# Stage two by halves of tokens, expert sums handed over bank by bank, and the pick table moved, in an eight-stage transformer kernel

## The reference, cut to what matters

```python
x = x + tanh(g_xattn[0]) * wkv(td, tf, layernorm(x), ctx)                  # L0 attention: a scan
x = x + tanh(g_ffn[0])   * moe8_top2_plus_shared(layernorm(x))             # L0 FFN
x = x + tanh(g_xattn[1]) * masked_softmax_attention(layernorm(x), ctx)     # L1 attention
x = x + tanh(g_ffn[1])   * L1_ffn(layernorm(x))                            # 32 experts, top 4
x = x + tanh(g_xattn[2]) * attention_32_heads(layernorm(x), ctx)           # L2 attention
x = x + tanh(g_ffn[2])   * dense_moe8(layernorm(x))                        # L2 FFN, 8 experts x 256
x = x + tanh(g_xattn[3]) * int8_attention_16_heads(layernorm(x), ctx)      # L3 attention
x = x + tanh(g_ffn[3])   * dense_moe8_top_p(layernorm(x))                  # L3 FFN, 8 experts x 512
```

## Time and profile before

| | before |
|---|---|
| median of 3 runs | 1008.02 us (1006.38 to 1008.49) |
| the profiled execution's own time | 1007.44 us |
| its span, first to last instruction | 1005.6 us |
| PE busy / weight load | 854.8 us (85%) / 529.0 us |
| DVE / ACT / POOL busy | 675.8 / 521.0 / 327.2 us |
| mean granted PE clock | 0.942 of full |

### The profile page before, as it was taken

How to read it: one execution, slowest core, us unless ns; L and a number is a source line. 1 busy time by engine, 2 the same in 40 slices (tenths; PEclk the granted TensorE clock), 3 DMA queues, 4 the chain that set the end, 5 groups by cost and what they waited for, 6 DMA issues and landing times.

```text
span 1005.6 us, 17167 instructions
## 1 busy us (share of the span) xinstructions
PE 854.8 (85%) x6369; PEld 529.0 (53%) x6369; DVE 675.8 (67%) x1402; ACT 521.0 (52%) x840; POOL 327.2 (33%) x267
## 2 busy tenths in 40 slices
PE   5977999867457877887988998789799899999997
PEld 3434665554335666564544554455455556555654
DVE  7995889778856777274345579767777657744444
ACT  4714345444336887155568743664456885523332
POOL 2531333322674555203035662101355334100000
PEclk9978999987768999897679999999999999999999
DMA  8974443310247776502013453111465445433332
GB/s 270 330 261 119 120 122 110 89 48 1 99 152 232 255 233 189 185 33 64 2 45 114 127 179 106 48 49 33 126 189 158 127 127 160 155 97 109 95 104 80
DMA packets 60191, 129.12 MB, mean 128 GB/s; under 512 B 9267, under 2 KB 25025, under 8 KB 60114
## 3 DMA queue, kind: packets, MB, share of 16 engines
q1 hardware_dynamic: 55506, 119.17, 38.6%
q0 software_dynamic: 4608, 8.94, 2.4%
HBM read 83.95 MB, written 48.27 MB: 131 GB/s over the span
## 4 chain that ended last, share of the span: by engine, by line
PE 42%; DVE 18%; issue 18%; POOL 8%; ACT 7%; DMA 5%; SPq 1%; POOLq 0%; DVEq 0%; ACTq 0%
PE ps L1465 15%; PE ps L1481 7%; DMA arena<-seats 4%; POOL W L770 3%; PE ps L1829 2%; PE ps L1552 2%; PE ps L1815 2%; DVE x L2318 2%; PE ps L1749 1%; POOL W L773 1%; PE ps L1408 1%; POOL arena L714 1%; PE ps L1567 1%; DVE stats L2036 1%; POOL wb L773 1%
## 5 line engine op out<-in xcount | busy, mean ns | idle before, releaser
L1465 PE MATMUL ps<-turned_buf,W 128*128 128x512 f16 x576 | 135.2, 385 | 4.0 <-ACT ctx_sb L1024 1.7
L2302 DVE SCALAR_TENSOR_TENSOR ctx_sb<-ps,ctx_sb 128x512 f32<-128x512 f32 x96 | 66.2, 689 | 102.8 <-PE ps L1465 75.7
L1465 PE MATMUL ps<-turned_buf,wb 128*128 128x512 f16 x576 | 132.6, 379 | 2.6 <-DVE ctx_sb L2302 2.0
L2309 DVE TENSOR_TENSOR ctxT<-ctx_sb,ctxT 128x512 f16<-128x512 f32 x96 | 69.6, 726 | 63.7 <-ACT ctxT L1032 63.2
L770 POOL TENSOR_SCALAR W<-W 128x768 f32<-128x768 f32 x32 | 69.3, 2167 | 129.3 <-ACT wb L1044 67.2
L1032 ACT ACTIVATE ctxT<-ctx_sb 128x512 f16<-128x512 f32 x96 | 60.2, 627 | 91.1 <-DVE ctx_sb L2302 90.9
L1024 ACT ACTIVATE ctx_sb<-ps 128x512 f32<-128x512 f32 x96 | 57.2, 596 | 96.3 <-PE ps L1465 96.1
L1465 PEld LDWEIGHTS ps<-turned_buf,W 128*128 128x128 f16 x576 | 55.9, 100 | 67.1 <-issue 7.1
L1408 PE MATMUL ps<-turned_buf,W 128*128 128x512 f16 x360 | 86.7, 394 | 2.5 <-issue 2.5
L1465 PEld LDWEIGHTS ps<-turned_buf,wb 128*128 128x128 f16 x576 | 55.4, 98 | 62.2 <-DVE ctx_sb L2302 3.0
L758 POOL DMA_INDIRECT slots<-arena x64 | 62.3, 973 | 49.4 <-ACT arena L1095 37.7
(11 more groups left out here) (411 smaller groups left out, 1704.9 us busy)
## 6 DMA issues: line engine op xcount, KB each, us to landing
W<-in_w SPq DMA_DIRECT2D x77, 384.0 KB, 3.6
seats<-k_st SPq DMA_DIRECT2D x8, 1152.0 KB, 10.9
arena<-seats SPq DMA_DIRECT2D x32, 288.0 KB
kept<-W SPq DMA_DIRECT2D x24, 384.0 KB, 4.1
kept<-wb SPq DMA_DIRECT2D x24, 384.0 KB, 4.2
W<-kept SPq DMA_DIRECT2D x24, 384.0 KB, 3.0
wb<-kept SPq DMA_DIRECT2D x24, 384.0 KB
wb<-in_w SPq DMA_DIRECT2D x18, 384.0 KB, 3.9
```

What stands on the lines that cost most here:

```text
L1465: last = nc.tensor.matmul(bank(4 + n), w4[k % 4][:, w, n * D + c * P:n * D + (c + 1) * P], x16[:, i, c, half * HALF:(half + 1) * HALF], st ...
L2302: nc.vector.scalar_tensor_tensor(h_g[:, g % 2, :], bank(5), 1.0 / WSCALE, h_s[:, g % 2, :], ALU.mult, ALU.mult).then_inc(sem("gated"), 1)
L2309: nc.vector.tensor_tensor(h_16[:, g % 2, 1, :], h_g[:, g % 2, :], h_16[:, g % 2, 0, :], ALU.subtract)\
```

## The change

1. **Stage two by halves.** Keys are turned in groups of 4, 2, 6, 4 instead of 6, 6, 4, the first four through banks 1 and 3 only; half 0 of xn goes to PE after them, then half 0's scores, then two keys, then half 1. DVE: add half 0, statistics 0, add half 1, normalise 0, statistics 1, normalise 1; then the four steps of half 0, down_lo and the mask's largest, sums 0, the four steps of half 1, add 0, statistics 0, sums 1, add 1, statistics 1. POOL casts the mask between the two powers.
2. **One power for the RMS norm.** DVE gives POOL the variance times (1 + 1e-6) plus 1e-11, so that one power makes `rms`; the plain `rstd`, needed later, is made from a second variance for all eight tiles after the norm.
3. **Places.** `m_cum + m_base` is added before the counts; the mask instruction joins the one that writes the places; m_to is made and signalled in halves of four tiles, and POOL starts after the first.
4. **Dense passes.** DVE signals `out_read` after two tiles and after four; PE waits for the first before bank 6 and for the second before bank 7.
5. **picks** moves from step 6 to step 0 of half 0, with a wait for all of L2 attention's results.
6. **Rounding** of the norm in L3 attention: two tiles in step 6 and two in step 7, instead of four in step 7.
7. **Stores**: half 1 of the result in two pieces of two tiles.
8. Semaphores are merged (names only).

```diff
-        KEY_BANKS = (0, 1, 2, 3, 0, 1, 4, 5, 6, 7, 4, 5, 6, 7, 4, 6)
-        KEY_GROUPS = (6, 12, 16)
+        KEY_BANKS = (1, 3, 1, 3, 0, 2, 4, 5, 6, 7, 4, 5, 6, 7, 4, 6)
+        KEY_GROUPS = (4, 6, 12, 16)
...
+            for lo, hi in ((0, 4), (4, 6), (6, 8)):
+                sp.wait_ge(sem("out_read"), 2 * (EXPERTS_AT[2 + lo // 4] + E3) - hi % 4 // 2)
+                sp.dma_start(out.rearrange("b s d -> s b d")[:, lo:hi, :], x[:, lo:hi, :]).then_inc(sem("out_done"), 16)
...
-                    if s == 3:
...
+                    into = rms if s == 3 else rstd
+                    nc.gpsimd.tensor_tensor(into[:, sl], veps[:, sl], mhalf[:, sl], ALU.pow).then_inc(sem("ln_rstd"), 1)
...
-            inv_sqrt(2)
+            inv_sqrt(2, (0,))
             link(nc.gpsimd.tensor_copy(a1_mask, mask8[:, :, :]))
             nc.gpsimd.tensor_scalar(a1_neg, a1_mask, -1.0, 1e30, ALU.add, ALU.mult).then_inc(sem("mask"), 1)
+            inv_sqrt(2, (1,))
             inv_sqrt(3)
+            pool.wait_ge(sem("plain_var"), 1)
+            nc.gpsimd.tensor_tensor(rstd[:, :], veps[:, :], mhalf[:, :], ALU.pow).then_inc(sem("plain_rstd"), 1)
-            pool.wait_ge(sem("seat"), 2)
             for i in range(TOP1):
                 for t in range(B):
+                    if i == 0 and t % 4 == 0:
+                        pool.wait_ge(sem("seat"), 2 + t // 4)
...
             def picks():
+                pool.wait_ge(sem("x_2"), B)
-                    if s == 6 and h == 0:
+                    if s == 0 and h == 0:
                         picks()
...
@@ ACT @@
+            turned(2, xT_of, (0,))
             down_hi(1, 0)
-            turned(2, xT_of)
+            for n in range(KEY_GROUPS[0], KEY_GROUPS[1]):
+                key_out(n)
+            turned(2, xT_of, (1,))
...
@@ PE, half_down @@
                 for t in range(4):
+                    if first and g and t % 2 == 0:
+                        pe.wait_ge(sem("out_read"), 2 * (EXPERTS_AT[p] + k // per) - 1 + t // 2)
@@ PE, stage two @@
-            pe.wait_ge(sem("key_ready"), KEY_GROUPS[0])
-            turn(2)
             for h in range(2):
+                if h:
+                    for n in range(KEY_GROUPS[0], KEY_GROUPS[1]):
+                        turn_keys(n)
+                    pe.wait_ge(sem("key_ready"), KEY_GROUPS[0])
+                turn(2, halves=(h,))
                 pe.wait_ge(sem("turned"), 2 * KD * 2 + KD * (h + 1))
...
+            pe.wait_ge(sem("key_ready"), KEY_GROUPS[1])
...
@@ DVE, half_add @@
-                ins.then_inc(sem("out_read"), 1)
+                    if t % 2:
+                        ins.then_inc(sem("out_read"), 1)
@@ DVE, stages two and three @@
-            layer_norm(2, add_ffn(0))
-            down_lo(1, 0)
+            link(add_ffn(0)(0))
+            statistics(2, 0)
+            link(add_ffn(0)(1))
+            normalised(2, 0)
+            statistics(2, 1)
+            normalised(2, 1)
+            dve.wait_ge(sem("xn_ready"), B * 3)
...
-            layer_norm(3, add_a1, scale=rms)
+            a1_arg(0)
+            down_lo(1, 0)
+            link(nc.vector.tensor_reduce(a1_s[:, 0, :], a1_mask, AX.X, ALU.max))
+            a1_sums(0)
+            a1_arg(1)
+            link(add_a1(0))
+            rms_statistics(0)
+            a1_sums(1)
+            link(add_a1(1))
+            rms_statistics(1)
+            normalised(3, 0, rms)
+            normalised(3, 1, rms)
+            dve.wait_ge(sem("xn_ready"), B * 4)
+            nc.vector.tensor_scalar(veps[:, :], mv[:, :, 1], LN_EPS, None, ALU.add).then_inc(sem("plain_var"), 1)
             x_lo(3, 1)
...
+            link(nc.vector.tensor_scalar(m_cum, m_cum, m_base, None, ALU.add))
...
-            link(nc.vector.tensor_scalar(m_place, m_kept, 0.0, None, ALU.is_gt))
-            nc.vector.scalar_tensor_tensor(x_rows[:, :, D:ROW], m_cum, m_base, m_place, ALU.add, ALU.mult)
...
+            nc.vector.scalar_tensor_tensor(x_rows[:, :, D:ROW], m_kept, 0.0, m_cum, ALU.is_gt, ALU.mult)
+            for h in range(2):
+                sl = slice(4 * h, 4 * h + 4)
...
...
-                    if s == 7:
-                        whole_round(xn[:, :, :], 0, sl)
+                    if s in (6, 7):
+                        whole_round(xn[:, :, :], 0, slice(4 * h + 2 * (s - 6), 4 * h + 2 * (s - 6) + 2))
```

More of the change, by code:

```diff
@@ L240, in build @@
         m_ones = ar.take([B, E1])
-        m_place = ar.take([B, E1])
         m_w = ar.take([B, TOP1])
@@ L842, in _, with turned @@
             nc.scalar.activation(wdec[:, :], td[:, :], ACT.Exp).then_inc(sem("gates"), 1)
-            def turned(s, dst, scale=None):
-                for half in range(2):
+            def turned(s, dst, halves=(0, 1)):
+                for half in halves:
                     act.wait_ge(sem("turn"), 2 * turns_before(s) + half + 1)
@@ L852, in turned @@
                             src = src.rearrange("p (b s) -> p b s", b=B // 2)
[L853 to L854 removed]
+                        nc.scalar.activation(o, src, ACT.Copy).then_inc(sem("turned"), 1)
             def turned_16(s, scale=None):
@@ L1156, in _ @@
                     .then_inc(sem("a1_pT"), 1)
-            for n in range(KEY_GROUPS[0], KEY_GROUPS[1]):
+            for n in range(KEY_GROUPS[1], KEY_GROUPS[2]):
                 key_out(n)
@@ L1162, in last_keys @@
             def last_keys():
-                for n in range(KEY_GROUPS[1], KEY_GROUPS[2]):
+                for n in range(KEY_GROUPS[2], KEY_GROUPS[3]):
                     key_out(n)
@@ L1363, in _, with turn @@
         def _(pe):
-            def turn(s, src=xn):
-                for t in range(B):
+            def turn(s, src=xn, halves=(0, 1)):
+                for t in range(4 * halves[0], 4 * halves[-1] + 4):
                     pe.wait_ge(sem("xn_ready"), B * s + t + 1)
@@ L1474, in half_down @@
                 pe.wait_ge(sem("h_lo"), HALVES + g + 1)
-                if first and g:
-                    pe.wait_ge(sem("out_read"), EXPERTS_AT[p] + k // per)
-                elif first:
+                if first and not g:
                     pe.wait_ge(sem("golden"), 1)
                 for t in range(4):
+                    if first and g and t % 2 == 0:
+                        pe.wait_ge(sem("out_read"), 2 * (EXPERTS_AT[p] + k // per) - 1 + t // 2)
                     for w, i in THREE:
@@ L1512, in shared @@
                 seat_numbers()
-                for n in range(KEY_GROUPS[1], KEY_GROUPS[2]):
+                for n in range(KEY_GROUPS[2], KEY_GROUPS[3]):
                     turn_keys(n)
-                pe.wait_ge(sem("key_ready"), KEY_GROUPS[2])
+                pe.wait_ge(sem("key_ready"), KEY_GROUPS[3])
                 pe.wait_ge(sem("seat"), 1)
@@ L1710, in _ @@
                 last.then_inc(sem("a1_pv"), 1)
-            for n in range(KEY_GROUPS[0], KEY_GROUPS[1]):
+            for n in range(KEY_GROUPS[1], KEY_GROUPS[2]):
                 turn_keys(n)
             turn(3, x_rms)
-            pe.wait_ge(sem("key_ready"), KEY_GROUPS[1])
+            pe.wait_ge(sem("key_ready"), KEY_GROUPS[2])
             router(1)
@@ L2383, in _, with a1_sums @@
                     .then_inc(sem("a1_arg"), 1)
-            for h in range(2):
+            def a1_sums(h):
                 rest, valid = mine(a1_s[:, 3, :], h), mine(a1_s[:, 0, :], h)
@@ L2396, in add_a1, with rms_statistics @@
                 return ins
-            layer_norm(3, add_a1, scale=rms)
+            def rms_statistics(h):
+                sl = range(4 * h, 4 * h + 4)
+                for t in sl:
+                    ins = nc.vector.bn_stats(stats[:, t, :], x[:, t, :])
+                link(ins)
+                for t in sl:
+                    ins = nc.vector.bn_aggr(mv[:, t, :], stats[:, t, :])
+                link(ins)
+                nc.vector.tensor_scalar(veps[:, 4 * h:4 * h + 4], mv[:, 4 * h:4 * h + 4, 1], 1.0 + RMS_EPS, LN_EPS * RMS_EPS,
+                                        ALU.mult, ALU.add).then_inc(sem("ln_var"), 1)
+            a1_arg(0)
[12 more added lines that the diff above has]
+            nc.vector.tensor_scalar(veps[:, :], mv[:, :, 1], LN_EPS, None, ALU.add).then_inc(sem("plain_var"), 1)
             x_lo(3, 1)
```

70 lines of the change are left out of this document (31 added, 39 removed).

## The result

In one comparison on one chip the changed kernel took 1002.45 us (median of 12 executions, 997.92 to 1005.60) and the kernel before 1008.73 (12 executions, 1004.23 to 1014.95). The ratio is 0.9932, 95% interval [0.9914, 0.9951]: 6.9 us less, 4.9 to 8.7. The forecast was 8.05 less. In a second comparison the same code gave 0.9912 [0.9883, 0.9941] (experiment `after_again`). The profiled execution took 1000.27 us with a span of 998.4, 7.2 shorter than before's 1005.6.

What follows compares the result with a forecast made beforehand. PE bounds pass 3, hand-overs between engines bound stages two and three; scatter -2.05, picks -1.0, dense passes -4.3 and stores -0.7 sum to -8.05, from 1007.44 to 999.4, median 1000.0, range 996.0 to 1006.0.

Steps and rivals of the forecast that it cites:

- rival B: Waits before pass 3 only change their name; passes 1, 2 and picks give nothing, 2.7 less gain, 1002.7; chance 0.15.
- Stage two (a): Half 0's norms end about 212.3, its scores begin at 213.9, DVE's mask steps at 217.4, 2.7 earlier.
- (b): Stage two, ACT's queue is late next, table load included; first exponential near 222.9, as before (222.97).
- (c): Stage two, DVE's steps from 217.4 through the last statistics end at 236.1, against 235.42 in the old order: +0.7.
- (d): RMS norm: one power replaces two powers and four products, -2.2; last norm starts at 237.5, 1.4 earlier.
- (e) Places: Before the scatter: one instruction fewer (0.33) and addresses after four maxima (0.42 earlier); -0.65 kept of 0.75.
- Scatter: Start of the first scatter, from stages two and three and places together: -2.05, bounds +0.7 and -4.0.
- picks: Around 600 us, POOL's pick table moved off DVE's rounding, rounding split: -1.0, bounds +0.5 and -1.8.
- Dense passes: Bank-by-bank hand-over: pass 2 -1.4, pass 1 -0.3, pass 3 -2.6, together -4.3, bounds -1.5 and -6.4.
- Rival A: Stage three: new gaps keep PE at 1.2 GHz through gate and up, counts 3.5 later, 1003.5; chance 0.12.
- C: Rival A and rival B at once, or ACT's queue takes back stage two's gain; 1005.5; chance 0.10.
- D: Experts' ring of copies, loads and turns settles at worse spacing, 3.75 instead of 3.40 us per expert; 1010.1; chance 0.08.

Runs made afterwards that it cites:

- `after_again`: The changed kernel once more, no edit, with a profile of its own; ratio to the kernel before 0.9912 [0.9883, 0.9941].
- `adds_by_bank`: Changed kernel, PE signalling bank 6 early so DVE adds its two tiles during bank 7; 847 us to last sum 153.21 against 153.87.
- Experiment 7: Changed kernel plus an unread one-column exponential on ACT, loading the table early; mask steps to exponential 3.89 instead of 4.61, to last norm 0.04 won.
- experiment 5: Changed kernel with part 2 undone (two powers, four products per half); last variance to last half's norm 3.73 against 1.52.
- `after`: The changed kernel in its first comparison and profile; median 1002.45 us, ratio to the kernel before 0.9932, profiled execution 1000.27 us.
- `exp_early`: The kernel of Experiment 7: changed kernel with the exponential's table loaded early; gate and up took 7.86.
- The three parts alone: Kernel before with only stages two, three and places, only the dense hand-over (ratio 0.9964), or only pick table and rounding (0.9995).
- experiment 2: Kernel before with only the bank-by-bank hand-over of the dense passes (`dense_alone`); ratio 0.9964 [0.9935, 0.9993].
- `dense_alone`: The kernel of experiment 2: kernel before with only the dense passes' bank-by-bank hand-over; ratio 0.9964, 847 us to last sum 153.87 against 156.34.

## Why the prediction was right, and where it was not

The time was right: 8.05 forecast, 6.9 (4.9 to 8.7) measured in one comparison and 0.9912, 8.9 us (6.0 to 11.8), in the second. The times alone don't tell the forecast from rival B, whose 5.3 less lies within the first interval; the stretches have to. By its steps, against the means of the repeats and not against the single pair:

- **Stage two (a).** Norms of half 0 beside POOL: 2.71 for four, ending at 212.2 (213.47 - 1.29), forecast 212.3. Mask steps 2.25 earlier, forecast 2.7. The missing 0.4 are PE's turn at half clock: the scores began at 214.3 and not 213.9, and then took the 3.5 that were forecast. Where the turn fell at full clock (`adds_by_bank`), it ended 0.46 earlier.
- **(b), (c).** The exponential came 0.5 earlier where none was forecast, the last variance came 0.33 later, forecast +0.7. The terms listed for (c) add up to 235.85 and not to 236.1, so they say +0.4; the forecast carried 0.25 too much. Experiment 7 shows that ACT's table load and PE's scores are both within 1 us of the path.
- **(d).** 2.21 against 2.2, shown by experiment 5. Last norm 1.9 earlier, forecast 1.4.
- **(e) Places.** The seat numbers start 2.41 earlier and the scatter 3.19: 0.78 between them, forecast 0.75 of which 0.65 were kept. Adding m_base under PE's counting was taken as free because DVE idled 0.96 there. In `after` DVE idled 0.14, since gate and up ended sooner; in `exp_early` it idled 1.57. The cover depends on the clock.
- **Scatter.** -2.05 forecast; -3.3 in three profiles, -1.3 in two, -2.5 in the mean.
- **picks.** -1.0 forecast, -1.5 measured: a mis-sized term. The forecast charged up to +0.5 for the table's new place and counted 1.4 of DVE's time only in part. At 595 us POOL's three instructions cost under 0.1, and everything that the rounding stalled was path. The marker of 0.34 in all eight failed in one (0.665).
- **Dense passes.** -4.3 forecast. Pass 3 -2.6: measured -2.47. Each long wait lost 0.79, forecast 0.75; the failure in it is the wait of 0.53, which can't give 0.75, balanced by the 0.73 that should have been 1.51 in before's profile. Passes 1 and 2 -1.7: measured about -1.15 with the dips taken out, of which the hand-over alone brings 0.3 to 0.6. Carrying 60% of the waits was too much: PE's waits fell by 2.4 us there. The longest of them, 1.58, only fell to 1.38, since DVE was late with its own work.
- **Stores.** -0.7 forecast, -0.83 measured.

With the means the sum is -2.5 - 1.5 - 1.15 - 2.5 - 0.8 = -8.45, less the 1 us that the experts may give back. That it comes so near to 8.05 is in part luck: the scatter and picks brought 1.0 more than forecast, the passes 0.7 less. The three parts alone sum to 0.36 + 0.05 + 0.14 = 0.55%, each uncertain by 0.25 to 0.3, too wide to show how the parts add. By stretches the hand-over and picks overlap by 0.65 between 600 and 637 us (experiment 2), and from 732 to 745 us the whole change has a gain that the hand-over alone lacks.

Rival B (the waits before pass 3 change their name; passes 1, 2 and picks give nothing) is wrong on picks, which gave 1.5, and half right on the passes: PE's waits fell from 4.8 to 2.4 us there and the stretch by 1.15. Pass 3's gain, in all nine profiles with the edit, says nothing against it, since B expected that too. In the pair of profiles alone B looked wholly true, since the changed kernel's stretch from 637 us was 1.04 longer; that was two dips of the clock in one and none in the other. Rival A happened in part and was priced too high: 2.0 in two of five. C did not happen, nor D. The prediction's main blind spot was that it took the profile of before as the kernel before. It is one draw, lucky by 1.54 from 847 us on and by 2.3 against the mean of the five profiles without part 4 in passes 1 and 2 (it has no dip there), unlucky by 3.0 in L2 attention.

## What to carry to other kernels

Before a difference of two profiles is explained, profile the same code again: whole stretches of unchanged code can differ by more than the change, and only what repeats (156.34 against 153.87 in every run) is the change's. Where PE sets the pace, as in pass 3, a hand-over of a buffer in two halves is worth the time of one half at each wait that is longer than that, and a boundary's weight load besides; make it in both directions where the sum ends the kernel. Where another engine sets the pace, a shorter wait is not a shorter kernel: `dense_alone` lost 3.0 us of PE's waits between 637 and 847 us and won 0.3. An instruction of POOL is worth moving away from DVE's instructions on the path where the two were seen to meet: four roundings took 2.77 beside it and 1.23 away from it.

## What the hardware showed that was not expected

Identical code from 431 to 552 us took 114.66 to 121.59 us, and the three profiles above 120 us are those with the lowest granted clock in it (PEclk 0.66 to 0.73 in 450 to 500, 0.76 to 0.83 in the other eleven). In the dense passes, with PE busy 46 of 50 us, a short dip came at the same point of the program, near 785 us of before's time, in nine of the fourteen profiles, in kernels with and without the edits. And a DVE instruction of 0.17 us on 128x4 elements took 1.38 beside a POOL instruction of 1.64.
